# Expert outputs weighted at the PSUM exit and summed into a DRAM copy of the residual by accumulating scatters

## The reference

```python
logits = x @ gate_w.T
probs = softmax(logits)
top_w, top_i = top_k(probs, 2)
top_w = top_w / sum(top_w)
out = 0
for e in range(12):
    h = silu(x @ w1[e].T) * (x @ w3[e].T)
    out = out + h @ w2[e].T * cw[:, e:e+1]      # cw: top_w scattered over the experts
x = layernorm(x + out)
```

## Time and profile before

| | us |
|---|---|
| median of 3 runs | 752.48 (749.74 to 755.52) |
| profiled execution, its own time | 752.41 |
| span of its records | 749.4 |
| TensorE busy | 716.7 |
| VectorE busy | 496.2 |
| ScalarE busy | 366.8 |
| GpSimd busy | 287.1 |

### The profile page before, as it was taken

The page is one execution under the profiler, slowest core; times in us unless marked ns, Lnnn a source line. Parts: engine busy times, 40 slices in busy tenths (PEclk is TensorE's granted clock), DMA queues, the critical chain, the costliest instruction groups (busy, mean ns, idle before and its releaser), DMA issues. The chain is left out here.

```text
span 749.4 us, 17438 instructions
## 1 busy us (share of the span) xinstructions
PE 716.7 (96%) x6219; PEld 522.7 (70%) x6219; DVE 496.2 (66%) x1103; ACT 366.8 (49%) x714; POOL 287.1 (38%) x254
## 2 busy tenths in 40 slices
PE   9999899999999999999998988999999999999994
PEld 4677778787777778677666877666666666666641
DVE  2857968879688786896868776544444444444477
ACT  3865654657556576676465111343333333333264
POOL 0574555564654636545511002233333333333110
PEclk9999999999999999999999879999999999999998
DMA  8824365353652535545310016555466665522955
GB/s 324 317 72 147 132 227 170 113 170 114 215 180 91 177 129 188 179 139 200 113 73 15 30 41 233 219 197 196 140 223 228 216 217 207 206 85 89 346 229 194
DMA packets 40139, 127.01 MB, mean 169 GB/s; under 512 B 4224, under 2 KB 4608, under 8 KB 38144
## 3 DMA queue, kind: packets, MB, share of 16 engines
q1 hardware_dynamic: 31024, 99.48, 37.9%
q0 software_dynamic: 6880, 22.55, 8.9%
q10 hardware_dynamic: 2160, 3.93, 1.4%
HBM read 81.12 MB, written 44.83 MB: 168 GB/s over the span
## 5 line engine op out<-in xcount | busy, mean ns | idle before, releaser
L1088 DVE COPY_PREDICATED ST<-msk,pS 128x256 f32<-128x256 uint8 x224 | 121.1, 570 | 55.4 <-issue 25.6
L763 POOL TENSOR_TENSOR piece_parts<-piece,piece_parts 128x1024 f16<-128x1024 f32 x48 | 103.6, 2160 | 97.8 <-ACT piece_parts L708 97.8
L1889 POOL DMA_INDIRECT y_scratch<-ysb,desti x43 | 42.4, 987 | 163.4 <-DVE ysb L1794 163.4
L1582 PE MATMUL pH<-ring,xgh 128*128 x344 | 103.0, 299 | 0.8 <-issue 0.4
L1583 PE MATMUL pH<-ring,xgh 128*128 x344 | 102.9, 299 | 0.0
L1584 PE MATMUL pH<-ring,xgl 128*128 x344 | 102.9, 299 | 0.0
L757 POOL TENSOR_TENSOR RL<-RL,AM 128x256 f32<-128x256 f32 x96 | 71.6, 746 | 73.5 <-ACT RL L700 67.5
L401 PE MATMUL pS<-RL 64*128 64x64 f32 (+2 forms) x1536 | 91.4, 269 | 0.0
L401 PEld LDWEIGHTS pS<-RL 64*128 64x128 f32 (+1 forms) x1536 | 86.7, 182 | 2.2
L1778 DVE TENSOR_TENSOR hid<-pH,sil 128x320 f32<-128x320 f32 x43 | 21.1, 492 | 95.9 <-ACT sil L1657 95.9
L741 DVE TENSOR_TENSOR RL<-RL,AM 128x256 f32<-128x256 f32 x96 | 70.4, 733 | 13.3 <-ACT RL L687 11.4
(11 more groups left out here) (251 smaller groups left out, 1537.2 us busy)
## 6 DMA issues: line engine op xcount, KB each, us to landing
piece<-in_w_experts SPq DMA_DIRECT2D x48, 512.0 KB, 4.8
w_split_scratch<-piece_parts SPq DMA_DIRECT2D x48, 512.0 KB, 3.8
ring<-w_split_scratch SPq DMA_DIRECT2D x12, 2048.0 KB
yin<-y_scratch SPq DMA_DIRECT2D x16, 512.0 KB, 12.1
out_x<-X SPq DMA_DIRECT2D x8, 512.0 KB, 2.8
x_scratch<-X ACTq DMA_DIRECT2D x15, 256.0 KB, 2.0
X<-in_x SPq DMA_DIRECT2D x2, 1536.0 KB, 18.2
RL<-in_wxT SPq DMA_DIRECT2D x4, 256.0 KB, 5.3
```

The costliest lines, as they stand in the source:

```text
L763: g.tensor_tensor(piece_parts[buf][:, 1, :], piece[buf][:, :], piece_parts[buf][:, 0, :], ALU.subtract).then_inc(piece_lo, 1)
L1088: v.copy_predicated(out[:, :, :, 0 if lv == 0 else 1, :], msk[:, lv, :, :].rearrange(shape, m=m), pS[:, :, lv * S:(lv + 1) * S].rearrange( ...
L1582: pe.matmul(p[:, 0, 0:F], xgh[par][:, k, :], wh, start=(k == 0), stop=False)
```

## The change

What it does:

- A second DRAM scratch, sum_d (2048 rows and 128 rows for padding), gets a copy of the normalised x: 15 more stores of 256 KB on ScalarE's queue in send_x2, and two on SP's queue ahead of the first weight load.
- The weights wtop are stored to DRAM (w_d, 4096 x 1 f32) in the order of the token-expert pairs, from the SP queue behind the loads of ring places 1 and 2.
- GpSimd gathers for each tile the 128 weights of its slots (`weigh`, 43 more indirect DMAs with 4-byte rows), using the new index tile wseli; desti now is the token's row.
- copy_out waits for this gather and multiplies by the weight instead of copying.
- send scatters with an addition in the DMA into sum_d. As a token has two rows to add, send i now waits until send i-1 has landed.
- The softmax steps stand ahead of tile 0 on both VectorE and ScalarE (on VectorE: subtractions after low_x(0), the six steps after low_x(1)).
- At the end SP loads sum_d into X as 16 pieces of 256 KB; the diagonals, the matmuls and the additions are gone, and VectorE's last phase starts with bn_stats.

```diff
             def send_x2(t):
                 a.wait_ge(norm2, t + 1)
                 a.dma_start(x2_d[t * P:(t + 1) * P, :], X[:, t, :]).then_inc(x2_out, 16)
+                a.dma_start(sum_d[t * P:(t + 1) * P, :], X[:, t, :]).then_inc(sum_in, 16)
...
             sp.dma_start(x2_d[last * P:, :], X[:, last, :]).then_inc(last_out, 16)
+            sp.dma_start(sum_d[last * P:T, :], X[:, last, :]).then_inc(last_sum, 16)
+            sp.dma_start(sum_d[T:, :], X[:, 0, :]).then_inc(last_sum, 16)
...
             for slot in range(1, RING):
                 load(slot, slot)
+            sp.wait_ge(wtop_ready, 1)
+            sp.dma_start(w_d.rearrange("(n p j) o -> p n (j o)", p=P, j=2), wtop[:, :, :]).then_inc(w_stored, 16)
...
-            yv = y_d[0:2 * T, :].rearrange("(n p j) c -> n p j c", p=P, j=2)
+            sp.wait_ge(x2_out, 16 * last)
+            sp.wait_ge(sum_in, 16 * last)
+            sp.wait_ge(last_out, 16)
+            sp.wait_ge(last_sum, 32)
             for i in range(NT):
-                sp.dma_start(yin[i % YIN][:, :, :], yv[i]).then_inc(y_in[i % YIN], 16)
+                sp.dma_start(X[:, i, :], sum_d[i * P:(i + 1) * P, :]).then_inc(y_in[i], 16)
...
             high_x(0, 0)
             high_x(1, 1)
-            tile(0, 0)
-            tile(1, 1)
             a.wait_ge(top_ready, 1)
             a.activation(probs[:, :, :], probs[:, :, :], ACT.Exp)
             a.activation(ptop[:, :, :], ptop[:, :, :], ACT.Exp).then_inc(exp_done, 1)
+            tile(0, 0)
+            tile(1, 1)
...
-            v.scalar_tensor_tensor(desti[:, :], secd[:, :], -2.0, padq[:, :], ALU.add, ALU.add).then_inc(dest_ready, 1)
+            v.tensor_scalar(wseli[:, :], secd[:, :], -2.0, 0.0, ALU.add, ALU.max)
+            v.scalar_tensor_tensor(desti[:, :], invq[:, :], -1.0, padq[:, :], ALU.add, ALU.add).then_inc(dest_ready, 1)
...
             def copy_out(i, j, par):
                 v.wait_ge(o_full, i + 2)
                 v.wait_ge(y_free[par], j + 1)
-                v.tensor_copy(ysb[par][:, :], pO[:, 0, :]).then_inc(o_out, 1)
+                v.wait_ge(wg_in[par], j * 16 + 16)
+                v.tensor_scalar(ysb[par][:, :], pO[:, 0, :], wgate[par][:, 0:1], None, ALU.mult).then_inc(o_out, 1)
...
+            def weigh(i):
+                par = i % 2
+                g.indirect_dma_start(out=wgate[par][:, :], out_offset=None, in_=w_d,
+                                     in_offset=bass.IndirectOffsetOnAxis(ap=wseli[:, i:i + 1], axis=0)).then_inc(wg_in[par], 16)
...
                 g.wait_ge(o_out, i + 2)
+                if i:
+                    g.wait_ge(y_sent[1 - par], (i + par) // 2 * 16)
                 g.sem_inc(g_waited, 1)
-                g.indirect_dma_start(out=y_d, out_offset=bass.IndirectOffsetOnAxis(ap=desti[:, i:i + 1], axis=0),
-                                     in_=ysb[par][:, :], in_offset=None).then_inc(y_sent[par], 16)
+                g.indirect_dma_start(out=sum_d, out_offset=bass.IndirectOffsetOnAxis(ap=desti[:, i:i + 1], axis=0),
+                                     in_=ysb[par][:, :], in_offset=None, compute_op=ALU.add).then_inc(y_sent[par], 16)
...
                 if i == 0:
                     g.wait_ge(dest_ready, 1)
+                    g.wait_ge(w_stored, 16)
+                    g.sem_inc(g_waited, 1)
+                    weigh(0)
+                    weigh(1)
+                    g.wait_ge(sum_in, 16 * last)
+                    g.wait_ge(last_sum, 32)
                 send(i)
+                if i + 2 < SLOTS:
+                    weigh(i + 2)
```

More of the change, by code:

```diff
@@ L132, in __init__ @@
         self.ones_h = take(P, F16)
-        self.diag = [early[:, i * 2 * P:(i + 1) * 2 * P].rearrange("p (c t) -> p c t", c=2) for i in range(NT - 3)]
 def attention(nc, X, idt, kc, gw, x, wxT, ww, wk, wv, wr, wo, by_feature, ident, masks, consts, gate_w, w_experts, w_split, logitT, early, pA,
-              x2_d, x2_out):
+              x2_d, x2_out, sum_d, sum_in):
     with ExitStack() as ctx:
@@ L1326 @@
 AHEAD = 4
-YIN = NT
 DVE_LAST = 2
 LAST_GROUPS = [(0, 4), (4, 8), (8, 12), (12, 14), (14, 16)]
-ON_DVE = (0, 6, 11)
-ON_PE = [i for i in range(NT) if i not in ON_DVE]
-MIX = 5
 K_WIDTHS = [E, SLOTS, P, 2 * NT, SLOTS, P, E * E, E]
@@ L1339, in kc_col, with experts @@
     return kc[:, K_AT[k]:K_AT[k + 1]]
-def experts(nc, X, idt, kc, gw, w_split, early, pA, x2_d, x2_out, y_d, out):
+def experts(nc, X, idt, kc, gw, w_split, early, pA, x2_d, x2_out, sum_d, sum_in, w_d, out):
     I32 = mybir.dt.int32
@@ L1397, in experts @@
         ysb = [sb(f"ysb{i}", [P, C]) for i in range(2)]
-        yin = [sb(f"yin{i}", [P, 2, C]) for i in range(YIN)]
+        wgate = [sb(f"wgate{i}", [P, 1]) for i in range(2)]
         stats = sb("stats3", [P, NT, 6])
@@ L1429, in experts @@
         last_out = sem("last_out")
+        last_sum = sem("last_sum")
+        w_stored = sem("w_stored")
+        wg_in = [sem(f"wg_in{i}") for i in range(2)]
         w_in = [sem(f"w2_in{i}") for i in range(RING)]
@@ L1446, in experts @@
         y_sent = [sem(f"y_sent{i}") for i in range(2)]
[L1447 to L1450, removed]
+        y_in = [sem(f"y_in{i}") for i in range(NT)]
         terms3 = sem("terms3")
@@ L1623, in _ @@
             down(SLOTS - 1, place(SLOTS - 1))
[L1624 to L1630, removed]
         @block.scalar
@@ L1676, in _ @@
                 tile(i, i % 2, more=i + 2 < SLOTS)
[L1678 to L1683, removed]
             for q, (lo, hi) in enumerate(LAST_GROUPS):
@@ L1804, in _ @@
             low_x(0, 0)
-            low_x(1, 1)
-            tile(0, None, 0)
             v.tensor_tensor(probs[:, :, :], ro.logit[:, :, :], ro.top[:, :, 0:1].broadcast_to([P, NT, E]), ALU.subtract)
             v.tensor_tensor(ptop[:, :, :], ro.top[:, :, 0:2], ro.top[:, :, 0:1].broadcast_to([P, NT, 2]), ALU.subtract).then_inc(top_ready, 1)
-            tile(1, 0, 1)
-            tile(2, 0, 0)
+            low_x(1, 1)
             v.wait_ge(exp_done, 1)
@@ L1819, in _ @@
                             psum_[:, :].rearrange("p (n o) -> p n o", o=1).broadcast_to([P, NT, 2]), ALU.mult).then_inc(wtop_ready, 1)
-            tile(3, 1, 1)
+            tile(0, None, 0)
+            tile(1, 0, 1)
             pairs = (SLOTS - 2) // 2
-            with v.Fori(2, pairs) as j:
+            with v.Fori(1, pairs) as j:
                 tile(j * 2, j - 1, 0)
@@ L1834, in terms @@
                 v.scalar_tensor_tensor(nmr[:, at], mv[:, at, 0], -1.0, rstd[:, at], ALU.mult, ALU.mult).then_inc(terms3, 1)
[L1836 to L1845, removed]
             def measure(i):
-                v.wait_ge(y_added, i + 1)
+                v.wait_ge(y_in[i], 16)
                 return v.bn_stats(stats[:, i, :], X[:, i, :])
@@ L1853, in _ @@
                 for i in range(lo, hi):
[L1854 to L1857, removed]
+                    ins = measure(i)
+                    if i == lo and q:
                         terms(q - 1)
-                step(measure(hi - 1))
+                step(ins)
                 for t in range(lo, hi):
@@ L1910, in program @@
     w_split = nc.dram_tensor("w_split_scratch", (E, P, 2, WCOLS), F16, kind="Internal").ap()
-    y_d = nc.dram_tensor("y_scratch", (2 * T + SLOTS * P, C), F32, kind="Internal").ap()
+    sum_d = nc.dram_tensor("sum_scratch", (T + P, C), F32, kind="Internal").ap()
+    w_d = nc.dram_tensor("w_scratch", (2 * T, 1), F32, kind="Internal").ap()
     with (nc.sbuf_tensor("X", [P, NT, C], F32) as X,
@@ L1917, in program @@
           nc.psum_tensor("pA", [P, 2, 512], F32) as pA,
-          nc.semaphore("x2_out") as x2_out):
+          nc.semaphore("x2_out") as x2_out, nc.semaphore("sum_in") as sum_in):
         attention(nc, X, idt, kc, gw, x, wxT, ww, wk, wv, wr, wo, by_feature, ident, masks, consts, gate_w, w_experts, w_split, logitT, early, pA,
-                  x2_d, x2_out)
-        experts(nc, X, idt, kc, gw, w_split, early, pA, x2_d, x2_out, y_d, out)
+                  x2_d, x2_out, sum_d, sum_in)
+        experts(nc, X, idt, kc, gw, w_split, early, pA, x2_d, x2_out, sum_d, sum_in, w_d, out)
 def constants():
@@ L1945, in constants @@
     packed = [np.broadcast_to(a, (P, n)) for a, n in zip(
-        [e, np.arange(SLOTS), np.arange(P), token, P * np.arange(SLOTS) + p + (2 * T + 2), p < np.arange(P), lower, p % GATE_W == e],
+        [e, np.arange(SLOTS), np.arange(P), token, p + (T + 1), p < np.arange(P), lower, p % GATE_W == e],
         K_WIDTHS)]
```

3 lines of the change are left out of this document (1 added, 2 removed).

## The result

The changed kernel takes 791.35 us (median of four runs, 788.59 to 793.13) where the kernel before, beside it, takes 752.05 (four runs, 749.74 to 755.52): ratio 1.0515, 95% interval 1.0464 to 1.0567. It is 5% slower. The forecast was 760.5 us with a range up to 787: the side was right, the size was not, and the time lies outside the range.

A forecast was written before the change was run, and what follows sets the result against it. TensorE was taken to bound the kernel up to 717 us, VectorE the end. From 752.4 us: -10.7 last phase, +10.8 store, +4 clock, +5 scatters gave 761.5, rounded to 760.5 us; range 744 to 787, the forecast's own 754 to 768.

The forecast's parts named there:

- The last phase: After the last tiles: VectorE's additions and products go, ScalarE becomes late; 10.7 us won, bounds 9 to 12.3.
- The store of the weights: Start: the store queues behind two ring loads and takes 6 us, so TensorE's second matmuls restart 10.8 us later.
- rival 4: Start: the store's runs of 8 bytes are dear, 18.8 to 21.5 us; kernel 774 to 777 us; chance 0.10.
- The clock: TensorE's wait of 8.8 us at the start makes the granted clock fall to half; 4 us lost, bounds 0 to 6.5.
- The scatters: Loop: chained adding sends land in 4.7 us, 8.3 beside each of nine ring loads; 5 us lost, rounded to 4.
- So 1.9 us of room: Loop: GpSimd's chain has 1.9 us of slack, leaving 0.6 us lost for each of nine ring loads.
- Rival 3: Loop: the scatter chain sets the period, landing in 6.6 us, 0.8 more per step; some 794 us; chance 0.15.
- Copy_out and the further gathers: Loop: copy_out with a factor stays 0.69 us, 43 more gathers of 1.3 us fit GpSimd's idle time; nothing added.

The follow-up runs named there:

- the two runs whose loop loses nothing: Changed kernel without the loop's nine ring loads: 762.09 us; changed kernel with plain scatters and no weight gathers in the loop: 760.60 us.
- the chained kernel before: The kernel before with one wait added, each send waiting until the send ahead has landed: 753.36 us, ratio 1.0025.

## Why the prediction was wrong, step by step

**The last phase** (-10.7 forecast, -11.7 measured): right, by its own steps: bn_stats first, then ScalarE late throughout; the four normalisations take 2.93 us as before. The loads of X didn't hide quite at nothing: on the padding tiles sends stood 7.5 and 8.9 us apart beside them, which is the +3.4 before copy_out(42).

**The store of the weights** (+10.8 forecast, for the restart of TensorE's second matmuls; +7.4 by that row, 479.02 to 487.71 less the first fetch's 1.3; +9.1 by copy_out(0)): right in kind and near in size, by luck in part, since two errors balanced. The data took some 2 us and not 6: the window 478 to 480. In exchange it moved later than "behind the loads at 476.4". The store was seen at about 482.3 (471.02 + 11.3), forecast 483.9; copy_out(0) came at 485.56, forecast 487.9. The picture of one queue in which nothing passes was too narrow: on a queue of its own it took longer. The estimate of 21.5 us for 2048 packets, worked out from a figure of the Trainium skill, page "DMA: Bandwidth & Descriptors", section "Bandwidth", was not borne out: rival 4 falls. That figure is of a transfer of 64 packets, from HBM to SBUF. In the run with the store on ScalarE's queue, q10 moved 2064 packets in 2.9% of 16 engines' time over 455 to 495 us: 0.009 us for each on its engine, some 1.2 us for 128 or 129 on each of 16 engines at once.

**The clock** (+4 forecast): the fall came in the wait where it was expected, 2.4 us into the 5.75 us, and its depth too (half). But it was at half for only some 6.8 us from 484.4, nearly half of it the wait itself. What it cost by itself isn't shown. The two terms together, 14.8 us forecast, cost 9.3 and 9.9 us in the two runs whose loop loses nothing, from the first fetch to copy_out(37); less the restart there (8.0 and 7.4) 1 to 3 us are left for the clock. The stretch of 14.4 us at low clock was taken from another stage and was too long here. That the clock would fall again in the loop, five times, was not in the forecast: it is part of what the scatters cost.

**The scatters** (+4 to +5 forecast, bounds 0 and 20; +35 measured): the step that failed. Its parts:
- The accumulating scatter by itself, taken at 4.7: measured 5.5 to 5.7, inside the bounds of 3.57 and 6.2.
- Beside a ring load 8.3 was taken, once per load: measured 6.8 to 10.8, 8.93 in the mean, and nine loads make ten such landings and three more late sends.
- "So 1.9 us of room": this was the real error. It is the slack inside one tile, and it was set against each ring load afresh, as though the chain were back in time by the next. A chain recovers only by the difference between the tile and its link. With 5.80 - 3.57 a late one is regained in a tile, as the chained kernel before shows; with 5.80 - 5.5 at best it takes ten tiles, and a ring load comes every four. The right sum takes the room off once: with landings that regain nothing, the forecast's own 8.3 would have given 9 x 2.5 - 1.9 = 21 us, and the measured thirteen periods of 8.63 give 37. TensorE's stops and its low clock behind them lie within these periods; they are no further term.
- What stands behind a waiting send was named (weigh and fetch follow it) and priced at nothing. They wait behind the ring load too (the gather over 8 us, the fetch 9.3). This turned out to be no loss of its own: earlier fetches, four buffers, or no gathers changed nothing while the chain set the pace. They are where TensorE shows the delay, not where it comes from.

**Rival 3** had the mechanism (the chain sets the period) and even the time, 794 us, but not the place: it asked for landings above 5.8 us in every tile. They stayed at 5.76 in 25 of 38, and the tiles lost nothing between ring loads. The mean landing decided, 256.2 / 38 = 6.7 us, not the single one. The Trainium skill, "Collectives: The Full Stack", section "Stop ④ — SDMA + CCE: where bytes move and the add happens", calls the addition free between two reads and a write. Here an adding scatter lands after 5.5 us against 3.57, with 64 packets more; the runs don't part the arithmetic from the second read, but the 4.2 us that the forecast drew from it did not come. With them there would have been room.

**Copy_out and the further gathers** at nothing: true as the forecast meant them (copy_out 0.75 us, no wait for GpSimd's time while the additions are there), but not beyond: the runs without the addition show that the gathers spoil the chain's recovery, some 19 us that the longer landings hide in the kernel after. "They would cost only if they ate the 0.4 us left before y_free" did not see this.

## What to carry to other kernels

Where a change makes every transfer wait for the former one, add up the landings over the whole loop, the slow ones beside bulk loads among them, and set the sum against the loop's time; slack within one step counts once, and a late chain comes back only by the difference between the step and a normal link. When two suspects each give back little singly, take both away in one run before acquitting either. And an own queue does not protect a small transfer from a burst; smaller bursts do, at the price of the burst's own pace.

## What the runs showed of the hardware

- A scatter of 128 rows of 2 KB with an addition lands 5.5 us after its row's start, a plain one in 3.5 to 3.6; its row on GpSimd takes 1.61 us against 0.99, and q0 has 11008 packets (15.9% of the engines' span) where the same kernel without the addition has 8256 (8.7%): 64 packets more for each of 43 scatters, and nearly double the transfer time.
- Beside a load of 2 MB on another queue: plain scatters 7.3 to 8.8 us (the chained kernel before), adding ones 6.8 to 10.8, a fetch of 128 rows 9.3, a gather of 512 bytes over 8. From 512 bytes to 256 KB the small transfer's size hardly shows; that of the load does (at most 7.8 us between sends beside pieces of 512 KB).
- The granted clock fell to half (1.2 GHz) in TensorE's waits of 3.7 to 5.75 us or up to 1.1 us behind their end, and stayed there for 3 to 4 us of work behind each: 9.4 us of the loop's 35.3.
- A store of 2048 runs of 8 bytes moves in about 2 us once its turn comes.
- Without the addition, six indirect DMAs issued by GpSimd without a pause (scatter, gather and fetch, twice) went with a silu on ScalarE some 3 us late, six times of six; four in a row (scatter and fetch, twice) did not, nor did nine fetches. Why is open.
